# Language-model tower on one core: turning the attention output and the normalised rows by transposing DMA instead of on TensorE

## What is computed

```python
h = _L0_tok_ref(x, emb_table, norm_weight, proj_weight)      # embed, RMS norm, project, RMS norm
h = h + _L0_attn_ref(_layernorm(h), Wq, Wk, Wv, Wo, gamma, beta)
h = h + _L0_ffn_ref(_layernorm(h), SU_ug, SU_dp, Wscale_ug, Wscale_dp, W_up, W_gate, W_down)

# attention: 16 heads of 32, q and k normalised per head
attn = jnp.einsum('bqhd,bkhd->bhqk', q, k) ** 2
attn = jnp.where(mask, attn, 0.0)                            # causal
o = jnp.einsum('bhqk,bkhd->bqhd', attn, v)
o = o / (jnp.swapaxes(jnp.sum(attn, -1), 1, 2)[..., None] + EPS)
return o.reshape(b, t, H * D) @ Wo.T

# feed-forward: inner width 2048, Walsh-Hadamard transform on both sides
x = fwht(x * SU_ug) / SCALE
x = silu(x @ W_gate.T * s_g) * (x @ W_up.T * s_u)
x = fwht(x * SU_dp) / SCALE
return x @ W_down.T * s_d
```

## Time and profile before

| | us |
|---|---|
| median of 3 runs (1417.93 to 1419.73) | 1418.95 |
| the profiled execution | 1420.2 |
| its span, first to last instruction | 1418.4 |
| PE busy | 1334.5 (94%) |
| DVE, ACT, POOL busy | 532.4, 458.0, 423.6 |

### The profile page before, as it was taken

The page is one execution under the profiler, slowest core; times in us unless marked ns, Lnnn a source line. Parts: engine busy times, 40 slices in busy tenths (PEclk is TensorE's granted clock), DMA queues, the critical chain, the costliest instruction groups (busy, mean ns, idle before and its releaser), DMA issues.

```text
span 1418.4 us, 20319 instructions
## 1 busy us (share of the span) xinstructions
PE 1334.5 (94%) x7993; PEld 676.7 (48%) x7993; DVE 532.4 (38%) x1049; ACT 458.0 (32%) x767; POOL 423.6 (30%) x371
## 2 busy tenths in 40 slices
PE   5575598999999999999999999999999999999999
PEld 3363255554444444454454444544445444544444
DVE  1655567654322343226222432234223523251110
ACT  4453564441233223332243123412333224312220
POOL 0342143332143313432244213420434124420210
PEclk9887799999999999999999999999999999999999
DMA  8900000000100010001000100001000100010000
GB/s 288 287 14 1 1 0 1 1 0 31 38 1 1 23 39 8 0 9 45 16 1 1 45 24 0 1 31 38 1 1 9 51 9 1 1 46 15 0 1 30
DMA packets 34125, 39.42 MB, mean 28 GB/s; under 512 B 6596, under 2 KB 23288, under 8 KB 33528
## 3 DMA queue, kind: packets, MB, share of 16 engines
q1 hardware_dynamic: 30528, 28.99, 6.3%
q0 software_dynamic: 2560, 8.39, 2.0%
q10 hardware_dynamic: 952, 0.75, 0.2%
HBM read 29.47 MB, written 8.65 MB: 27 GB/s over the span
## 4 chain that ended last, share of the span: by engine, by line
PE 89%; DVE 5%; ACT 3%; issue 1%; POOL 1%; DMA 1%; SPq 0%; DVEq 0%; ACTq 0%
PE bank L1067 25%; PE bank L1068 25%; PE bank L1069 25%; PE bank L1219 3%; PE bank L1062 2%; PE bank L1204 2%; PE bank L1205 2%; PE bank L1229 1%; PE bank L1110 1%; PE bank L1239 1%; DMA hid<-in_L_tok_norm_weight 1%; PE bank L1060 1%; DVE wgu L457 1%; PE bank L1247 0%; PE bank L1248 0%
## 5 line engine op out<-in xcount | busy, mean ns | idle before, releaser
L1067 PE MATMUL bank<-xT,wgu 128*128 128x512 f16 x1024 | 389.0, 380 | 1.4 <-DVE xT L688 1.4
L1069 PE MATMUL bank<-xT,wgu 128*128 128x512 f16 x1024 | 389.1, 380 | 0.0
L1068 PE MATMUL bank<-xT,wgu 128*128 128x512 f16 x1024 | 389.1, 380 | 0.0
L378 POOL TENSOR_TENSOR hid<-a,hid 128x512 f16<-128x512 f32 x128 | 147.9, 1155 | 526.1 <-ACT hid L835 526.1
L723 DVE SCALAR_TENSOR_TENSOR a<-bank,kap,sg 128x512 f32<-128x512 f32 x128 | 96.1, 751 | 486.0 <-PE bank L1069 334.8
L1068 PE MATMUL bank<-wd,hid 128*128 128x512 f16 x512 | 194.0, 379 | 0.0
L1069 PE MATMUL bank<-wd,hid 128*128 128x512 f16 x512 | 194.0, 379 | 0.0
L1067 PE MATMUL bank<-wd,hid 128*128 128x512 f16 x512 | 194.0, 379 | 0.0
L338 POOL TENSOR_TENSOR p<-prod,p 128x512 f16<-128x512 f32 x128 | 153.2, 1199 | 135.8 <-ACT p L835 135.7
L835 ACT ACTIVATE hid<-a 128x512 f16<-128x512 f32 x128 | 80.6, 630 | 278.8 <-DVE a L723 278.8
L1069 PEld LDWEIGHTS bank<-xT,wgu 128*128 128x128 f16 x1024 | 100.3, 98 | 121.5 <-issue 1.1
(11 more groups left out here) (183 smaller groups left out, 1389.5 us busy)
## 6 DMA issues: line engine op xcount, KB each, us to landing
out<-a SPq DMA_DIRECT2D x24, 256.0 KB, 2.1
wgu<-in_L_ffn_W_gate SPq DMA_DIRECT2D x16, 256.0 KB, 5.5
wgu<-in_L_ffn_W_up SPq DMA_DIRECT2D x16, 256.0 KB, 4.8
wd<-in_L_ffn_W_down SPq DMA_DIRECT2D x4, 1024.0 KB, 9.9
ids_b<-in_x SPq DMA_DIRECT2D x8, 256.0 KB, 4.2
out<-h_row SPq DMA_DIRECT2D x8, 256.0 KB, 2.0
xT<-in_L_tok_proj_weight SPq DMA_DIRECT2D x1, 1024.0 KB, 8.5
p<-in_L_attn_Wq SPq DMA_DIRECT2D x1, 1024.0 KB, 14.4
```

Source lines behind the costliest of these rows:

```text
L378: nc.gpsimd.tensor_tensor(hid[:, 1, s, :], a32[:, :], hid[:, 0, s, :], ALU.subtract)\
L1067: mm(dst, w[0], v[0], start=first, stop=False)
L1068: mm(dst, w[0], v[1], start=False, stop=False)
L1069: return mm(dst, w[1], v[0], start=False, stop=final)
```

## The change

SP issues a transposing DMA for each quad's `o16` and for each row group's `x16`, in all eight blocks, 64 in all. The PE transposes and the ACT copies behind them are gone. `oT` changes its order of axes so that one transfer fills one quad's part. ACT's next high half waits for the landing of the transfer before (in place of the flip); PE's sums wait for DVE's division in place of the oT copy; WO and mix wait for the landing. POOL's gather of `h_row` waits for WO of row group 0 in place of the last o flip. SP's loop over the blocks is written out. In SP's queue the o turns of a block stand ahead of the stores of the block before it, x turn 0 ahead of store 0, and x turn m+1 behind store m; in block 0 all eight turns stand ahead of the load of `ids_c`.

```diff
         oT: [P, 2, QUADS, T]  ->  [P, QUADS, 2, T]

+            def o_turn(n, q):
+                if n and q == 0:
+                    sp.wait_ge(S["wo_ready"], 4 * n)
+                sp.wait_ge(S["ol_done"], QUADS * n + q + 1)
+                nc.sync.dma_start_transpose(oT[:, q, :, :].rearrange("p l (m t) -> p (l m) t", t=P),
+                                            o16.rearrange("p l d -> p (l d)")).then_inc(S["oT_done"], 16)
+
+            def x_turn(n, m):
+                sp.wait_ge(S["xl_done"], 4 * n + m + 1)
+                if n or m:
+                    sp.wait_ge(S["xhada_ready"], 4 * n + m)
+                nc.sync.dma_start_transpose(xn16.rearrange("p (k t) -> p k t", t=P),
+                                            x16.rearrange("p l d -> p (l d)")).then_inc(S["xc_done"], 16)
+
+            def block_io(b, n, turning):
+                for q in range(QUADS):
+                    if turning is not None:
+                        o_turn(turning, q)
+                if turning is not None:
+                    x_turn(turning, 0)
                 for m in range(4):
...
                     nc.sync.dma_start(out_rows[b, m, :, :], o_out[m][:, :])\
                         .then_inc(S["stored"], 16)
+                    if turning is not None and m < 3:
+                        x_turn(turning, m + 1)
 
             load_ids_rows(1)
+            for q in range(QUADS):
+                o_turn(0, q)
+            for m in range(4):
+                x_turn(0, m)
             load_ids_columns(1)
-            with sp.Fori(0, NB - 2) as b:
-                block_io(b, b + 2)
-            block_io(NB - 2, None)
-            block_io(NB - 1, None)
+            for b in range(NB):
+                block_io(b, b + 2 if b + 2 < NB else None, b + 1 if b + 1 < NB else None)
...
   POOL, before the gather of h_row
-                    pool.wait_ge(S["o_flipped"], QUADS * n + QUADS)
+                    pool.wait_ge(S["wo_ready"], 4 * n + 1)
...
   ACT, before the high half of o16
+                    if not (isinstance(n, int) and n == 0 and q == 0):
+                        act.wait_ge(S["oT_done"], 16 * (QUADS * n + q))
   ACT, the copies at O_FLIP_AT and X_FLIP_AT
-                    copy(oT[:, :, q, :], banks[6][:, :].bitcast(F16).rearrange("p (l t) -> p l t", l=2))\
-                        .then_inc(S["oT_done"], 1)
-                    copy(xn16, PICK[0][:, :].bitcast(F16)).then_inc(S["xc_done"], 1)
   ACT, before the high half of x16
-                    act.wait_ge(S["flip_ready"], 4 * n + m)
+                    if not (isinstance(n, int) and n == 0 and m == 0):
+                        act.wait_ge(S["xc_done"], 16 * (4 * n + m))
...
   PE, before the sums
-                    pe.wait_ge(S["oT_done"], QUADS * n + q)
+                    if not (isinstance(n, int) and n == 0 and q == 0):
+                        pe.wait_ge(S["o_done"], QUADS * n + q)
   PE, the transposes at O_FLIP_AT and X_FLIP_AT
-                            last = nc.tensor.transpose(bank[:, c:c + P], o16[:, l, m * P:(m + 1) * P], ident16)
-                            last = nc.tensor.transpose(bank[:, c:c + P], x16[:, i, k * P:(k + 1) * P], ident16)
   PE, before mix m and before WO(0)
-                    pe.wait_ge(S["xc_done"], 4 * n + m + 1)
+                    pe.wait_ge(S["xc_done"], 16 * (4 * n + m + 1))
-                        pe.wait_ge(S["oT_done"], QUADS * n + QUADS)
+                        pe.wait_ge(S["oT_done"], 16 * (QUADS * n + QUADS))
```

More of the change, by code:

```diff
@@ L36 @@
 SUMS_AT = (4, 8, 12, 15)
-O_FLIP_AT = (5, 9, 13, 17)
 ROWS_AT = (17, 19, 21, 23)
@@ L40 @@
 X_LOW_AT = (20, 22, 24, 26)
-X_FLIP_AT = (21, 23, 25, 27)
 X_MIX_AT = (23, 25, 27, 29)
@@ L116, in tower @@
         h1 = sb("h1", [P, 2, 4, D])
-        oT = sb("oT", [P, 2, QUADS, T], F16)
+        oT = sb("oT", [P, QUADS, 2, T], F16)
         prod = sb("prod", [P, 2, T])
@@ L206, in tower @@
         onehotT_ready onehot_ready count_ready count_copied picked p_done ph_done pl_done
-        heads_ready den_done rden_done o_done oh_done ol_done o_flipped oT_done
+        heads_ready den_done rden_done o_done oh_done ol_done oT_done
         wo_ready h1_done bn_done mv_done ve_done rstd_done xs_done xa_done xm_done xh_done xl_done
-        flip_ready xc_done xhada_ready xThi_done xT_done
+        xc_done xhada_ready xThi_done xT_done
         gate_ready up_ready silu_done a_done ah_done al_done y_ready y_done y_last_done""".split()
@@ L266, in load_ids_rows @@
                 sp.wait_ge(S["onehotT_ready"], n)
-                nc.sync.dma_start(ids_b[:, :], x_rows[bass.ds(n, 1), :].broadcast_to([P, T])).then_inc(S["ids_land"], 16)
+                nc.sync.dma_start(ids_b[:, :], x_rows[n:n + 1, :].broadcast_to([P, T])).then_inc(S["ids_land"], 16)
             def load_ids_columns(n):
@@ L271, in load_ids_columns @@
                 sp.wait_ge(S["hrow_land"], 64 * n)
-                nc.sync.dma_start(ids_c[:, :], x_cols[bass.ds(n, 1), :, :].rearrange("a p c -> (a p) c"))\
-                    .then_inc(S["idc_land"], 16)
-            def block_io(b, n):
+                nc.sync.dma_start(ids_c[:, :], x_cols[n, :, :]).then_inc(S["idc_land"], 16)
+            def o_turn(n, q):
[16 more added lines that the diff above has]
+                    x_turn(turning, 0)
                 for m in range(4):
@@ L286, in block_io @@
                         sp.wait_ge(S["y_last_done"], b + 1)
-                    nc.sync.dma_start(out_rows[bass.ds(b, 1), m, :, :].rearrange("a p d -> (a p) d"), o_out[m][:, :])\
+                    nc.sync.dma_start(out_rows[b, m, :, :], o_out[m][:, :])\
                         .then_inc(S["stored"], 16)
+                    if turning is not None and m < 3:
+                        x_turn(turning, m + 1)
             load_ids_rows(1)
+            for q in range(QUADS):
+                o_turn(0, q)
+            for m in range(4):
+                x_turn(0, m)
             load_ids_columns(1)
-            with sp.Fori(0, NB - 2) as b:
-                block_io(b, b + 2)
-            block_io(NB - 2, None)
-            block_io(NB - 1, None)
+            for b in range(NB):
+                block_io(b, b + 2 if b + 2 < NB else None, b + 1 if b + 1 < NB else None)
             sp.wait_ge(S["stored"], 16 * 4 * NB)
@@ L1221, in attend @@
                     last.then_inc(S["heads_ready"], 1)
[L1222 to L1228, removed]
-                            last = nc.tensor.transpose(bank[:, c:c + P], o16[:, l, m * P:(m + 1) * P], ident16)
[L1230 to L1238, removed]
-                            last = nc.tensor.transpose(bank[:, c:c + P], x16[:, i, k * P:(k + 1) * P], ident16)
-                    last.then_inc(S["flip_ready"], 1)
                 if s in X_MIX_AT:
                     m = X_MIX_AT.index(s)
-                    pe.wait_ge(S["xc_done"], 4 * n + m + 1)
+                    pe.wait_ge(S["xc_done"], 16 * (4 * n + m + 1))
                     pe.wait_ge(S["xT_done"], 4 * n + m)
@@ L1257, in attend @@
                     for k in range(DC):
-                        last = split_mm(WOUT[m % 2][:, :], [oT[:, i, k, c] for i in range(2)],
+                        last = split_mm(WOUT[m % 2][:, :], [oT[:, k, i, c] for i in range(2)],
                                         [wo_t[:, i, k, :] for i in range(2)], k == 0, k == DC - 1)
```

9 lines of the change are left out of this document (removed).

## The result

The changed kernel takes 1402.48 us (median of 4 runs, 1400.20 to 1404.11) where the kernel before takes 1418.44 (4 runs, 1415.86 to 1419.73). The ratio is 0.9889, 95% interval 0.9866 to 0.9911: 1.1% faster, where 1437 and slower was forecast. A second set, of 6 runs, gave 1401.23 and a ratio of 0.9887 (0.9865 to 0.9908).

The account below looks back on a forecast made before the run. PE bounds blocks 1 to 7, engine hand-overs block 0. At L = 5: -24.6 + 7 x 6.0 + 0.5 = +17.9 on 1420.2, so 1438.1, or about 1437 as median; 8 in 10 range 1390 to 1550.

Parts of the forecast that it names:

- L: Time from SyncE's issue of a turn to the waiting engine seeing it landed; taken as 5.0 us, bounds 2.4 and 16.6.
- short case: Rival: a turn costs what a store of the same bytes costs, L about 3; 1394 us, chance 0.32.
- Removed: Transpose groups taken off PE in the seven blocks beside a feed-forward: 56 x 0.44 = 24.6 us won.
- (a): Last o turn of a steady tail, ahead of WO(0): stall L - 4.3 = 0.7 us.
- (b): h_row gather now waits for WO(0) in each steady tail: h1(0) 3.5 us late, but hidden before mix 0.
- (c): Mixes 1 and 2 of a steady tail, with single xn16 and x16 buffers: no stall, then 2.7 us.
- (d): Mix 3 of a steady tail, turn 3 queued behind row group 2's store: stall L - 2.4 = 2.6 us.
- Loads behind turns: ids_b and ids_c, issued by SP behind turns 2 and 3, land before the next block's DVE reads them: no cost.
- Block 0: First block's attention: 4.1 us won at three flip waits, turns in series; net +0.5 us at L = 5.0.
- long case: Rival: a turn's eight blocks move one after another or their issue holds SP, L about 8; about 1570 us, chance 0.27.
- break-even of 4.4: The L in us at which the change neither gains nor loses, with stalls of 3.7 a tail and block 0 at -2.4.
- likeliest case: The forecast itself, L 4.5 to 6.5, slower than before: own range 1422 to 1520 us, chance 0.36.

Follow-up runs that it names:

- the added transfers: Changed kernel with seven waited-for transfers (transposes of 1, 2, 4, 8 blocks, three plain copies) behind its last store, three times over; the twelve transposes landed in 2.2 to 3.1 us.
- the kernel in which PE waits for nothing: Changed kernel with turn 3 ahead of store 2, xT copy ahead of x_high, and the h_row gather issued earlier: 1388.35 us, 0.9790 of before.
- the early gather: h_row gather waits for the last o turn's landing instead of WO(0): 1406.69 us on the only-o-by-DMA kernel, 1388.35 on the changed kernel with both reorderings.
- the edits that these steps name: Against the changed kernel: turn 3 ahead of store 2 in SP's queue, 1396.27 us; xT copy ahead of x_high on ACT, 1396.30 us; both, 1388.58 us.

## Why the prediction was wrong

**The step that failed** is the value of L: "I put it a little above the ids_b row, the nearest, and take L = 5.0". It measured 3.1. The bounds, 2.4 and 16.6, held it. Three things put it too high. First, ids_b's 4.2 counts from the start of the issue, and I added 0.4 of issue to it again. Second, I added another 0.4 for "eight pieces of 128 fp16, 256 bytes each", a guess without a row. Third, the row itself: ids_b reads from HBM, 128 times the same row, while a turn stays within SBUF, where the added transfers show a plain copy of 256 KB landing in 2.3 us, as the store does (2.1 and 2.2), and the turning 0.8 more. The first two alone decided the sign. By the prediction's own steps L = 4.2, the row as it stands, gives stalls of 0 + 1.15 + 1.8 a tail and about -3 in block 0: some 7 us faster, about 1412. L = 4.6 gives some 5 us slower, and L = 5.0 the forecast.

In the prediction's own arithmetic the step from L = 5.0 to 3.1 is worth 42 us (+17.9 to -24.5). Against its short case the tails cost 1.1 a block and not 0.75 (2.6 in seven), and block 0 won 2.9 and not 5.2 (2.3): -19.6, and the two profiled executions differ by 20.0. The medians differ by 16.0; single runs lie up to 4 us apart in either kernel, and nothing here separates the rest from that. Against the medians the forecast missed by 1437 - 1402.5 = 34.5.

**The price of a turn beside the two pages cited.** The turn lands in 3.1 us, where the store takes 2.2 and a copy within SBUF 2.3. The Trainium skill, "VectorE: DVE Perf Modes", The three transpose paths, gives 1309 ns for one 128 x 128 by the DMA crossbar. One block alone took 2.2 us here, landing included, and eight in one transfer 3.1: the page's figure does not add up within a transfer, as the estimate of 10.5 us in the prediction let it. Over separate transfers something near it does add up, 1.24 us of issue each. The Trainium skill's "Advanced Engine Details and Errata", X-Bar Transpose (TRN2), as fast as regular DMAs, was the better guide; the trace agrees but for 0.8 us.

**Removed**, 24.6: right, 0.44 a group (3.52 us a block in the kernel in which PE waits for nothing), so 24.6 over seven blocks.

**(a)** At L = 3.1 it says no stall, and there is none: in the tail that ends at 524 the last o turn is issued at 470.95 and WO(0) starts at 475.21, 4.26 later, as the step's L - 4.3 has it.

**(b)** h1(0) starts 4.3 us behind the end of WO(0) (482.30 against 477.96), where it was 0.5 before: 3.8 late, forecast 3.5. Hidden, as forecast, and shown so by the early gather. What I hadn't seen is that the x turns hide it; with flips on PE it costs.

**(c)** Right in its chain: from the issue of turn 2 to mix 2 it takes L + 2.15 (654.93 to 660.18), forecast L + 2.25. At short L turn 2 is no longer held by DVE's finish but by mix 1 itself, 0.67 behind it; the rival's working had that and 0.1 us of stall, measured 0.3.

**(d)** Right: L - 2.4 = 0.7 at L = 3.1, measured 0.65; turn 3 goes out 2.7 behind mix 2's end, forecast 2.8. Both stalls vanish on the edits that these steps name.

**Loads behind turns** cost nothing: with all waits at the mixes gone, PE's wait view of the steady stretch shows none for them.

**Block 0**, forecast -5.2 for short turns, measured -2.9. The step that is off is "I take 1.4 x 3 = 4.1 won". The timeline of the changed kernel (the wait ahead of the last sums, the last o half, its turn, WO(0)):

```profile
118.75 1.56 PE L1231 MATMUL bank<-val,p 128*128 128x33 f16 x48 [3.80 <-POOL p L358]
122.39 1.15 POOL L379 TENSOR_TENSOR h_row<-wide,h_row 128x512 f16<-128x512 f32 x1 [3.70 <-ACT h_row L855]
123.57 1.23 SPq L276 DMA_TRANSPOSE oT<-h_row  x1
...
126.65 0.61 PE L1078 MATMUL bank<-wo_t,oT 128*128 128x512 f16 x1 [6.35 <-DMA oT<-h_row]
```

The waits at the flips are gone, and the sums wait longer for POOL in their place: up to 170 us it is 6.1 us in four waits, against 4.3 before. Counted from the first sums the last o half is ready 43.5 us behind them, against 45.0: 1.5 won, not 4.1. POOL's products set that pace, not the flips. Then the turn costs 0.9 more than flip and copy did (3.1 against 2.2), and the x tail wins the rest: from turn 0 at 137.16 to the feed at 162.75 it is 25.6, against 28.1 from x low to feed before (138.65 to 166.79), as the short case's steps have it (3.05 + 3 x 4.4 + 9.9 = 26.2). In that tail three mixes still wait for DVE's xT or the turn (4.1, 5.8 and 3.2 us before their starts at 149.24, 156.07 and 160.30).

**The chances.** The long case had 0.27 and the short 0.32 although both rows of 256 KB that I had quoted, 2.1 and 4.2 us, lie under the break-even of 4.4 when they are read as they stand, and of the rows quoted only the 1 MB load lies near the long case's 8 or above; of a turn's own price only the page's figure spoke for it. The upper half of the range, to 1550, came from there. The time fell into that range, near its lower end, and outside the likeliest case's own, 1422 to 1520.

**What stays open.** Some turns land late: one of the 32 x turns of the changed kernel took 3.8, the slowest of another kernel 4.9, and with block 0 on PE the last o turn took 4.7 in block after block. The trace shows what goes along with it. The view of the DMA side of that last o turn, from 772.5 to 777.3 us (queue, kind: packets, MB, share):

```profile
q8 instruction: 1, 0.02, 1.2%
...
oT<-h_row SPq DMA_TRANSPOSE x1, 4.7
```

and of the same turn in the changed kernel, from 770.5 to 775.3 us, where no packet of an instruction queue is listed:

```profile
q1 hardware_dynamic: 1056, 0.26, 28.3%
...
oT<-h_row SPq DMA_TRANSPOSE x1, 3.0
```

Packets of 8 or 16 KB of an instruction queue run through all traces, 15 to 31 us apart on average. In the ten kernels with whole turns, the probe left out, the traces give the landing of 508 turns. Of the 39 that took over 3.35 us, 38 had such a packet in flight while they moved; of the other 469, 23 had. So late turns go with these packets, which by the name of their kind load the program's own instructions, and in another kernel they come at other moments. That the one delays the other is likely; no experiment separated it.

## What to carry to other kernels

Moving turns of 128 x 128 blocks from TensorE to a transposing DMA pays where TensorE is the bound and the turned data is wanted more than some 3 us later: put as many blocks as possible into one transfer, since each transfer holds its queue for some 1.2 us whatever its size. Then look at what now stands behind the landing. Here two reorderings without any new work, turn 3 ahead of a store and the xT copy ahead of the high half, gave another 12.7 us, nearly as much as the change itself; that version, at 1388.6 (0.9795 of before), is the best of those measured, with the early gather equal to it. And when one unknown duration decides the sign, find out from where a column counts before anything is added to it, add no surcharge without a row, rank the neighbouring rows by the path of the data (within SBUF, to HBM, from HBM) as well as by their size, and give the bounds their chances by rows.

## What the runs showed of the hardware that I had not expected

- The issue of a transposing transfer takes 1.13 to 1.34 us on SyncE in the changed kernel and the added transfers, for one block of 128 columns as for eight; a plain one, behind the start-up, takes 0.33 to 0.64.
- Its landing grows little with its size: 2.2 to 2.3 us after the issue's start for one block, 2.4 for four, 3.1 for eight (256 KB); a plain copy of those bytes within SBUF takes 2.3.
- Little is lost behind a landing: an engine that waits for a turn starts 3.1 us after the issue's start (663.29 to 666.44 and 123.57 to 126.65).
- The load ids_b lands in 3.5 us in the changed kernel and 4.2 before, with the same bytes; no experiment was made on it.
- Turns that land late (over 3.35 us) go with an 8 or 16 KB packet of an instruction queue in flight: 38 of 39, against 23 of the 469 others.
